# Attention kernel on one NeuronCore: the two parts of a group's maxima are made, and transposed, behind the first two maxima of the next group

## The reference, cut to what matters

```python
q = _split_heads(query @ wq.T + bq, B, S)          # 16 heads of 16 channels
k = _split_heads(key @ wk.T + bk, B, S)
v = _split_heads(value @ wv.T + bv, B, S)
scores = jnp.einsum('bhqd,bhkd->bhqk', q, k) / math.sqrt(D_K)
...
p_attn = jax.nn.softmax(scores, axis=-1)
x = jnp.einsum('bhqk,bhkd->bhqd', p_attn, v)
```

## Time and profile before

| | us |
|---|---|
| three timed runs, median | 1637.36 |
| lowest, highest | 1636.45, 1640.37 |
| the profiled execution, own time | 1638.76 |
| its span in the trace | 1636.8 |

### The profile page before, as it was taken

One profiled execution on the slowest core, in us unless ns is written; L12 is line 12 of the kernel. 1 busy time (PEld: TensorE's weight loads), 2 busy tenths in 40 slices (PEclk: granted clock), 3 DMA queues, 4 the chain that ended last, 5 costly groups with the idle time before them and its releaser, 6 DMA issues. The chain is left out here.

```text
span 1636.8 us, 29399 instructions
## 1 busy us (share of the span) xinstructions
PE 1461.8 (89%) x10910; PEld 952.2 (58%) x10910; DVE 1287.1 (79%) x2140; ACT 1012.0 (62%) x1750; POOL 637.2 (39%) x957
## 2 busy tenths in 40 slices
PE   7989999999994399999999999869979999999846
PEld 6853333333483299999999999745533333333534
DVE  6889999999575766666665564379889999999687
ACT  5648999999642144444444444335549999999544
POOL 4315555556031234344442332255425555553120
PEclk9989999999995599999999999979979999999976
DMA  9975555555262122222222221168845555554103
GB/s 288 331 207 110 128 127 129 127 126 127 85 234 87 45 62 90 73 84 94 68 81 91 73 80 36 45 197 291 245 93 125 127 124 128 127 126 103 34 0 103
DMA packets 118748, 198.64 MB, mean 121 GB/s; under 512 B 29568, under 2 KB 63680, under 8 KB 117584
## 3 DMA queue, kind: packets, MB, share of 16 engines
q1 hardware_dynamic: 83840, 111.22, 22.3%
q0 software_dynamic: 33360, 83.94, 20.5%
q10 hardware_dynamic: 1408, 1.61, 0.3%
HBM read 117.77 MB, written 77.87 MB: 120 GB/s over the span
## 5 line engine op out<-in xcount | busy, mean ns | idle before, releaser
L1141 ACT ACTIVATE i_room<-a_ring 128x512 f32<-128x512 f32 x1024 | 550.5, 605 | 61.2 <-PE a_ring L1077 13.8
L349 DVE TENSOR_REDUCE logit<-a_ring 128x2 f32<-128x1024 f32 x416 | 488.3, 1217 | 3.5 <-PE a_ring L343 3.5
L1088 PE MATMUL a_pout<-i_room,values 128*17 128x256 f32 x4096 | 309.4, 386 | 3.3 <-ACT i_room L1141 1.8
L1779 ACT ACTIVATE e_full<-e_pH,b1T 128x320 f32<-128x320 f32 x256 | 135.0, 527 | 246.6 <-PE e_pH L1720 235.8
L1728 PE MATMUL e_pY<-fc_w,e_hid_hi 128*128 128x512 f32 x640 | 237.2, 407 | 0.5 <-DVE e_hid_lo L1832 0.5
L1077 PE MATMUL a_ring<-i_qk 64*128 64x512 f32 x768 | 193.9, 503 | 19.0 <-DVE logit L349 16.3
L1729 PE MATMUL e_pY<-fc_w,e_hid_lo 128*128 128x256 f32 x640 | 179.9, 281 | 0.0
L1077 PEld LDWEIGHTS a_ring<-i_qk 64*128 64x128 f32 x768 | 72.6, 186 | 182.9 <-DVE logit L349 134.2
L1088 PEld LDWEIGHTS a_pout<-i_room,values 128*17 128x17 f32 x4096 | 74.7, 96 | 175.7 <-ACT i_room L1141 136.9
L1840 POOL DMA_INDIRECT w<-normed,slot_get x80 | 84.1, 1052 | 225.7 <-PE fc_turned L1705 199.5
L1832 DVE TENSOR_TENSOR e_hid_lo<-e_full,e_hid_hi 128x640 fp32r<-128x640 f32 x128 | 119.6, 934 | 55.7 <-ACT e_hid_hi L1788 55.7
(11 more groups left out here) (335 smaller groups left out, 2583.4 us busy)
## 6 DMA issues: line engine op xcount, KB each, us to landing
ks<-i_room SPq DMA_DIRECT2D x64, 256.0 KB, 4.1
outs<-a_osb SPq DMA_DIRECT2D x64, 256.0 KB, 3.4
qs<-i_room SPq DMA_DIRECT2D x60, 256.0 KB, 5.2
fc_raw<-in_L_ffn_fc_w SPq DMA_DIRECT2D x15, 1024.0 KB, 5.3
i_qk<-ks POOLq DMA_DIRECT2D x84, 128.0 KB, 3.4
i_qk<-qs POOLq DMA_DIRECT2D x84, 128.0 KB, 3.6
BIG<-outs SPq DMA_DIRECT2D x64, 128.0 KB
ytok<-r_zeros SPq DMA_DIRECT2D x8, 1024.0 KB, 10.3
```

The source lines that it names most:

```text
L349: return e.tensor_reduce(nmax[:, :].rearrange("p (x y t) -> p x y t", x=2, y=2)[:, :, p, t], pair[:, :, :], AX.X, ALU.max, negate=True)
L1088: mm = e.matmul(pout[32 * h:32 * h + VW, at], v[:, b * TPB + t, g * HG + h, :], pexp[t][:, h, at], start=(t == 0 and half == 0), stop=(t = ...
L1141: e.activation(pexp[t][:, 2 * p + hh, :], score_bank(n * U + i, hh), ACT.Exp).then_inc(exped, 1)
L1779: e.activation(full[s % 2][:, h * WIDE:(h + 1) * WIDE], pH[h][:, 0:WIDE], ACT.Silu, bias=S.b1T[:, n * KF + f:n * KF + f + 1]).then_inc(act, 1)
```

## The change

Before, all three instructions stand behind the reduction of the last unit (place 7) of their group, and ahead of the first reduction of the next group. Now the CAST stands behind the reduction of place 0 of the next group, and the TENSOR_TENSOR and the STREAM_TRANSPOSE behind that of place 1. For the last group (31), which has no next one, all three stand behind its last reduction as before. The maxima of group 0 are turned before `attention` begins, and are not touched.

```diff
+                def cut_maxima(n, part):
+                    halves, whole = max_halves(nparts[n % 2]), max_whole(nmax[n % 2])
+                    if part == HI:
+                        e.wait_ge(reduced, (n + 1) * U - AHEAD)
+                        e.tensor_copy(halves[:, :, 0, :], whole).then_inc(cut, 1)
+                    else:
+                        e.wait_ge(cut, 2 * n - 1)
+                        e.tensor_tensor(halves[:, :, 1, :], whole, halves[:, :, 0, :], ALU.subtract).then_inc(cut, 1)
+
                 def turn_maxima(n):
-                    halves, whole = max_halves(nparts[n % 2]), max_whole(nmax[n % 2])
-                    e.wait_ge(reduced, (n + 1) * U - AHEAD)
-                    e.tensor_copy(halves[:, :, 0, :], whole).then_inc(cut, 1)
-                    e.wait_ge(cut, 2 * n - 1)
-                    e.tensor_tensor(halves[:, :, 1, :], whole, halves[:, :, 0, :], ALU.subtract).then_inc(cut, 1)
                     if n >= 3:
                         e.wait_ge(mrow[(n - 2) % G], moved(n - 2))
                     e.wait_ge(cut, 2 * n)
...
                 for m in range(AHEAD, NG * U):
                     reduce(m)
-                    if m % U == U - 1:
-                        turn_maxima(m // U)
+                    if m >= 2 * U and m % U == 0:
+                        cut_maxima(m // U - 1, HI)
+                    if m >= 2 * U and m % U == 1:
+                        cut_maxima(m // U - 1, LO)
+                        turn_maxima(m // U - 1)
+                for part in (HI, LO):
+                    cut_maxima(NG - 1, part)
+                turn_maxima(NG - 1)
```

## The result

The changed kernel takes **1677.14 us** (median of 4 runs, 1673.59 to 1680.08) against 1637.09 us for the kernel before (4 runs): ratio **1.0234, interval 1.022 to 1.0249** (a ratio is taken over all single runs and can differ a little from the quotient of the two medians, here 1.0245). The forecast was 1639.2 with a range of 1634 to 1647. The profiled execution took 1680.08 us with a span of 1678.1 us, 41.3 us more than the span of before; it was the slowest of the four, so its parts add up to a little more than the 40.05 us between the medians. It is read here in the same order: page, stretches, waits of PE, timelines.

A forecast was written before the change was run, and what follows sets the result against it. In the attentions PE, VectorE and ScalarE were taken as nearly full, with one 0.39 us PE wait per group. Groups +2.4 us, first group −0.5, moves nothing: +1.9 on 1637.36 gives 1639.2 us, range 1634 to 1647.

The forecast's parts named there:

- step 3: Third step of a group: PE's wait for a reduction goes, ScalarE's exponential then holds the product; gain 0.08 us, not 0.43.
- step 5: Sixth score of a group: a new 0.11 us wait for VectorE's place 2 reduction; net +0.03 us per plain group.
- The CAST is free: Behind the place 0 reduction: the CAST runs in VectorE's gap while the place 1 reduction waits for its product; no cost.
- The moves: SyncE's moves of the maxima: issued later, slack falls from 7.2 to 4.8 us, they take 3.4 to 4.3; cost nothing.
- the work behind the moves: On SyncE, the store of the outputs and two loads slip by 2.5 us; their waiters come two groups later.
- second rival: The moves land late before a group's first score, in a quarter of the groups: +10 us, 1649 us; chance 0.05.
- first rival: The TENSOR_TENSOR doesn't overlap the reduction in front: 0.12 us more in 58 groups, +8.9 in total, 1646 us; chance 0.15.
- a group with two halves: Group whose reduction in two halves (1.28 us instead of 1.22) falls at place 1 or 2: +0.09 us each, 9 per layer.
- The term for group 0 of layer 0: PE's 0.77 us wait at the third step of layer 0's first group shrinks; taken as −0.5 us.
- Rival 3: VectorE is quicker at step 5, so PE sets it: −0.08 us in 58 groups, floor 1632.3 us; chance 0.09.

The follow-up runs named there:

- e3: The changed kernel with SyncE's store of the previous group's outputs put ahead of the moves of the maxima: 1665.67 us, ratio 1.0155.
- e1: The changed kernel without GpSimd's eight additions of the output bias in layer 0 (left out of the result): 1649.06 us, ratio 1.0065.
- e2: The changed kernel with each GpSimd addition held until place 6 of the group is about to be scored: 1650.83 us, ratio 1.0073.
- e4: The changed kernel with the edits of e2 and e3 together, additions held and store ahead of the moves: 1638.31 us, ratio 0.9998.
- e7: The kernel before, with all three small instructions behind the reduction of place 0 of the next group: 1635.14 us, ratio 0.9976.

## Why the prediction was wrong

**The step that failed is one that was never made.** The parts on step 3 and step 5 walk through VectorE's row and ask of each small instruction what PE waits for; "The CAST is free", one of them says, since it runs in a gap of VectorE. The CAST and the TENSOR_TENSOR were taken at the length of their old place. The forecast did not ask what else runs on the core at the instruction's new time. GpSimd's row was called unchanged, and it was; its addition of 2.39 us, eight times in layer 0, now ran where the CAST or the TENSOR_TENSOR stood. The trace of before showed that addition 2 us behind the transpose, and the small instructions moved by 1.2 to 2.5 us. The eight groups are 2.0 to 5.2 us longer each in the change; the meetings are 28.9 us of scores in e3 and 26.4 to 26.9 between the change and e1 or e2. About two thirds of it is PE's wait for the delayed instruction (17.8 us in the change, 18.5 in e3). The rest is TensorE's lower clock, behind seven of the eight waits in e3 and six in the change, as e3's group 6 against its seven others shows: 1.4 to 1.5 us each.

**"The moves" failed as well.** The forecast costed them at nothing: "Those loads … are nearly over by then". The slack was right (4.8 us), and e3 and e4 show that it is enough. Two readings failed. The loads are not nearly over: the trace of before has the last one issued at 323.81, 1.0 us ahead of the forecast's 324.80, and it takes 3.7 us to land, until 2.8 us behind it. Its row:

```profile
323.81 0.51 POOL L426 DMA_DIRECT2D a_q<-qs  x1
```

The other is the sentence on the work behind the moves: the store and the load back "slip by 2.5 us, and who waits for them does so two groups later". Nobody waits for them, but they are traffic: 2.5 us later they meet GpSimd's loads (3.4 to 4.2 us each), which then run into the moves. It costs 5.5 to 7.7 us a layer, 13.1 us in e2's scores; e3's order takes it away. This is the second rival, "the moves land late", at 1649 us and a chance of 0.05: the run with this cause alone (e2) took 1650.83. Its chance was too low, since its own row, the slowest moves of 5.5 us, showed the collision. That its price came so near is in part luck: it took a quarter of the 58 groups as late, and in e2 twenty are.

**"Step 3: the wait goes, and ScalarE's takes its place": right.** The product of step 3 has its weights 335.34 − 334.07 = 1.27 us behind the score of step 2, released by ScalarE, as forecast. The score of step 3 itself comes 0.57 us behind that of step 2 (334.64 − 334.07), 0.1 sooner than forecast, which changes nothing, since the product behind it waits.

**"Step 5: a new wait for VectorE": right in size.** The TENSOR_TENSOR starts at 335.99, 0.09 us before the reduction in front ends (336.08), so the first rival falls. From that end to the next reduction's start it is 0.31 us (forecast 0.33), the group 10.09 (10.11), and a group with two halves at place 1 or 2 takes 10.15 to 10.17, +0.07 to +0.09 (+0.09). The term for group 0 of layer 0 (−0.5 us) came out smaller: 12.22 us in the change and 12.34 in e4, against 12.50. The whole sum of +1.9 us is what e4 tested: 1638.31 against 1639.14, no difference that can be told.

**Rival 3, VectorE quicker at step 5:** not so in the change, but its floor can be had in another place, as e7 shows.

So the forecast was good for the loop that it looked at, and 38.8 us (1677.14 − 1638.31) were lost outside it: some 27 to the additions, some 12 to the moves.

## What to carry to other kernels

Before a small VectorE instruction on SBUF is moved, list what GpSimd computes on SBUF within some microseconds of its new time, and what the instructions behind it in the DMA queues will then run beside; an unchanged row on another engine is no evidence of an unchanged meeting. When one instruction of 0.16 us can take 3 us, price the stall together with TensorE's clock behind it. A gap in which the engine waits for its input anyway, here the one behind the first reduction, is the place for small work; the further back it goes, the less slack its consumers keep (7.2 us ahead of the first score before, 6.1 in e7, 4.8 in the change).

## What the hardware showed that was not expected

- A CAST that the trace records as starting up to 0.9 us **before** the addition's recorded start also lasted to its end (group 18: 0.52 us before, 2.93 us long). The Trainium skill, "SBUF — State Buffer", section "Who interferes with whom", says that whoever issues first holds the ports. By the recorded starts VectorE was first and still waited, so either the recorded start of GpSimd's instruction lags its hold, or the CAST holds nothing when it starts; no run here tells these apart. Four CASTs that started 0.42 to 0.89 us before the addition were held. One that started 1.3 us before and ended 1.15 us before was not (group 6). GpSimd's loads, issued directly ahead of the addition, are not the cause: in e1, without additions, 56 CASTs ran beside such issues and none lasted over 0.28 us.
- A meeting of 2.1 to 3.3 us makes its group 2.0 to 5.2 us longer. In e3 PE idles 2.30 to 2.37 us at each of the eight; behind seven of these waits the granted clock falls to the lower level (0.61 over 4.4 us in group 10), behind one it stays at 1.00.
- The CAST alone lasts 0.25 us in its place before and 0.17 in the new one, with the same operands.
